# Graph layer on one core: the 64-byte tensor of exponents is allocated behind the statistics instead of ahead of the masks

## What is computed

```python
h = jnp.maximum(_layernorm(x, axis=-1), 0.0)
# in the layer, with _direction(x, W, Wg, b, bg, adj, rel_ids):
h = x @ W.T
g = h @ Wg.T
vals = (h[:, :, None, :] + b) * jax.nn.sigmoid(g[:, :, None, :] + bg)
onehot = (adj[..., None] == rel_ids).astype(h.dtype)
return jnp.einsum('bnmr,bmrd->bnd', onehot, vals)
# three directions (fwd, bwd: relations 2 to 40; loop: relation 1, on adj transposed)
x = x + jax.nn.relu(out)
```

## The kernel before

| tensor | bytes per partition | starts at | remainder by 128 |
|---|---|---|---|
| `x_all`, `adj_all`, `xn`, `hT_hi`, `hT_lo`, `gate` | 65536, 65536, 8192, 4096, 4096, 4096 | 16512 for `x_all`, the rest behind it | 0 |
| `vals` | 4096 | 168064 | 0 |
| `minus_half` | 64 | 172160 | 0 |
| `mask` | 8192 | 172224 | 64 |
| `stats` | 768 | 180416 | 64 |
| `var_eps`, `rstd`, `mean_neg` | 256 each | 181184, 181440, 181696 | 64 |
| `ident`, `ones`, `w_raw`, `w_gT`, `w_hi`, `w_lo`, `bias_all`, `zeros`, `bias_row`, `junk` | 512 to 8192 | 181952 for `ident`, the rest behind it | 64 |

## Time and profile before

### The profile page before, as it was taken

The page is one execution under the profiler, slowest core; times in us unless marked ns, Lnnn a source line. Parts: engine busy times, 40 slices in busy tenths (PEclk is TensorE's granted clock), DMA queues, the critical chain, the costliest instruction groups (busy, mean ns, idle before and its releaser), DMA issues.

```text
span 102.4 us, 2495 instructions
## 1 busy us (share of the span) xinstructions
PE 96.5 (94%) x802; PEld 92.5 (90%) x802; DVE 90.3 (88%) x197; ACT 90.3 (88%) x148; POOL 83.8 (82%) x158
## 2 busy tenths in 40 slices
PE   5988899999999999999999999999999999999960
PEld 2657798999999999999999999999999999999950
DVE  2289899999999999999999999999998588877661
ACT  5068889989999999999999989998999989898890
POOL 2275999999999999999999999999999999960000
PEclk9999999999999999999999999999999999999999
DMA  2899999999999999999999999999933341506345
GB/s 63 249 313 292 293 290 290 293 294 288 274 313 304 321 321 324 301 324 333 335 328 333 317 339 322 304 312 312 315 100 109 92 113 55 156 15 197 102 137 170
DMA packets 50288, 25.45 MB, mean 249 GB/s; under 512 B 866, under 2 KB 50276, under 8 KB 50276
## 3 DMA queue, kind: packets, MB, share of 16 engines
q1 hardware_dynamic: 50000, 25.17, 88.0%
q10 hardware_dynamic: 276, 0.13, 0.4%
HBM read 16.91 MB, written 8.39 MB: 247 GB/s over the span
## 4 chain that ended last, share of the span: by engine, by line
PE 80%; DMA 7%; DVE 4%; SPq 3%; ACT 3%; issue 1%
PE psum L827 25%; PE psum L805 14%; PE psum L806 14%; PE psum L810 14%; PE psum L792 13%; DMA x_all<-in_x 7%; ACT junk L467 2%; SPq L253 2%; DVE stats L554 1%; DVE xn L571 1%; DVE vals L587 1%; DVE hT_lo L597 1%; SPq L269 0%; SPq L270 0%; ACT gate L461 0%
## 5 line engine op out<-in xcount | busy, mean ns | idle before, releaser
L366 POOL TENSOR_SCALAR xn<-x_all,mean_neg,rstd 128x128 f32<-128x128 f32 x96 | 42.4, 456 | 0.5 <-issue 0.3
L805 PE MATMUL psum<-w_hi,hT_hi 128*128 128x256 f32 x128 | 34.3, 301 | 0.7 <-ACT hT_hi L427 0.3
L434 ACT ACTIVATE psum<-bias_all 128x1024 f32<-128x1024 f32 x32 | 33.0, 1032 | 0.7 <-DVE vals L587 0.6
L827 PE MATMUL psum<-vals,mask 128*128 128x128 f32 x256 | 33.6, 275 | 0.0
L806 PE MATMUL psum<-w_lo,hT_hi 128*128 128x256 f32 x128 | 31.6, 280 | 0.0
L827 PEld LDWEIGHTS psum<-vals,mask 128*128 128x128 f32 x256 | 31.1, 191 | 0.0
L554 DVE BATCH_NORM_STATS2 stats<-x_all 128x6 f32<-128x256 f32 x64 | 24.0, 420 | 3.5 <-DMA x_all<-in_x 3.5
L587 DVE TENSOR_TENSOR vals<-psum,gate 128x512 f32<-128x512 f32 (+1 forms) x33 | 21.9, 665 | 4.0 <-ACT gate L461 3.8
L805 PEld LDWEIGHTS psum<-w_hi,hT_hi 128*128 128x128 f32 x128 | 24.1, 188 | 1.5 <-issue 0.9
L348 POOL TENSOR_TENSOR rstd<-var_eps,minus_half 128x16 f32<-128x16 f32 (+2 forms) x11 | 24.5, 2224 | 0.1
L806 PEld LDWEIGHTS psum<-w_lo,hT_hi 128*128 128x128 f32 x128 | 24.2, 189 | 0.0
(11 more groups left out here) (38 smaller groups left out, 34.5 us busy)
## 6 DMA issues: line engine op xcount, KB each, us to landing
adj_all<-in_adj SPq DMA_DIRECT2D x16, 512.0 KB, 6.5
x_all<-in_x SPq DMA_DIRECT2D x15, 512.0 KB, 6.7
out<-x_all SPq DMA_DIRECT2D x14, 512.0 KB, 6.3
out<-x_all SPq DMA_DIRECT2D x3, 256.0 KB, 2.3
x_all<-in_x SPq DMA_DIRECT2D x2, 256.0 KB, 3.0
out<-x_all ACTq DMA_DIRECT2D x1, 128.0 KB, 2.5
out<-x_all SPq DMA_DIRECT2D x1, 128.0 KB, 2.6
w_raw<-in_L_gnn_W_loop SPq DMA_DIRECT2D x1, 64.0 KB, 2.4
```

The source lines that it names most:

```text
L366: last = pool.tensor_scalar(xn[:, g % XN, j * D:j * D + D], x_all[:, g * GC + j * D:g * GC + j * D + D], mean_neg[:, b % BATCH_SLOTS, k:k ...
L434: nc.scalar.activation(prod_ps[s].rearrange("p g a d -> p g (a d)"), bias_all[:, :, :].rearrange("p a d -> p (a d)").unsqueeze(1) .to_broa ...
L805: nc.tensor.matmul(to, hi, w_hi[:, :], start=False, stop=False, skip_group_check=True)
L827: last = nc.tensor.matmul(to[:, j * D:j * D + D], mask[:, g % MASKS, j * N:j * N + N], vals[:, s, j * D:j * D + D], start=True, stop=True)
```

## The change

One `sb(...)` line moves down by five lines. `minus_half` is no longer allocated between `vals` and `mask` but behind `mean_neg`.

```diff
         gate = sb("gate", [128, 2, GC])
         vals = sb("vals", [128, 2, GC])
-
-        minus_half = sb("minus_half", [128, BATCH])
         mask = sb("mask", [128, MASKS, GROUP * N])
         stats = sb("stats", [128, BATCH_SLOTS, BATCH // 2, 6])
         var_eps = sb("var_eps", [128, BATCH_SLOTS, BATCH])
         rstd = sb("rstd", [128, BATCH_SLOTS, BATCH])
         mean_neg = sb("mean_neg", [128, BATCH_SLOTS, BATCH])
+        minus_half = sb("minus_half", [128, BATCH])
         ident = sb("ident", [128, 128])
```

## The result

| | before | after |
|---|---|---|
| median | 104.19 us (7 runs) | 103.30 us (7 runs, 102.89 to 104.02) |
| ratio | | 0.9922, 95% interval 0.9903 to 0.9941 |
| the profiled execution | 104.14 us | 104.02 us |
| span in the profile | 102.4 us | 102.2 us |

The change makes the kernel 0.8% faster. The prediction named the masks' new place as worth nothing and forecast the old time, 104.3 us, so it is wrong, although 103.3 us lies within its range.

A forecast was written before the change was run, and what follows sets the result against it. The prediction took the pace at which PE starts its records as the bound. All terms were 0: 104.14 + 0 us against the profiled execution, 104.29 + 0 = 104.3 us as median, range 103.2 to 104.9 us.

The forecast's parts named there:

- the masks' new place: Masks at remainder 0 instead of 64, for PE's loads and ACT's and POOL's writes: forecast to change the time by 0.
- ACT's and POOL's masks: Writes of `mask`: term 0, staying at 640 ns on ACT and 0.61 us on POOL.
- the powers: POOL's powers for the statistics of each batch: 2.90 us each in slots at either remainder, term 0.
- the statistics' place: Slots of stats, var_eps, rstd and mean_neg only swap which has which remainder: term 0 on both ends.
- The slower rival: Aggregation: both operands at one remainder get into each other's way, 7.0 ns per record, 1.8 us, 106.1 us; chance 0.10.
- The last sign of being wrong: Profile after: wrong if PE's pace moves in any line, above all one whose operands did not move.
- The change part by part: Pricing of four kinds of access to moved tensors, each by its time at remainder 0 against 64; sum 0.
- PE's loads of `mask`: 256 aggregation loads, 191 ns against 188 at remainder 0, hidden behind multiplies: term 0, bounds 1.1 us gain, 1.8 us cost.
- the faster rival: Aggregation: loads of `mask` set its pace and remainder 0 frees it, 0.8 us, 103.5 us, at most 1.1 us; chance 0.14.
- slowest pace of the steady state: The products' 118 ns per record, used to price the loads' bad end and the slower rival at 1.8 us.
- The limit by the other engines: Steady state: POOL needs 10.84 us for four groups where PE needs 10.97, so the faster rival ends at 103.2 us.
- no change: Whole kernel: time the same within about 0.5%, what a measurement can tell; chance 0.76.

The follow-up runs named there:

- c2_stats_clean: Kernel before with stats, var_eps and rstd moved to remainder 0, mean_neg to the end; masks, ident and weights stay: 104.35 us, ratio 0.9991.
- c1_after_copy: The changed kernel unchanged, timed once more against the kernel before: 103.65 us, ratio 0.9936.
- c5_read_0: Kernel before, with PE loading the aggregation's stationary operand from an unchanging tensor of ones at remainder 0, masks still written at 64: 103.44 us, ratio 0.9907.
- c3_light_after: Changed kernel with less work: ACT's test reads 128 of 1024 columns, DVE's late statistics and POOL's late powers halved: 103.11 us, ratio 0.9879 to before.
- c1_mask_only: Kernel before with only the masks moved to remainder 0, statistics and all behind them staying in place: 103.38 us, ratio 0.9917.
- c5_read_64: Kernel before, with PE loading the aggregation's stationary operand from an unchanging tensor of ones at remainder 64, masks still written at 64: 104.35 us, ratio 1.0006.
- c1_stats_only: Kernel before with the statistics moved to remainder 0 and masks kept; its second gap also moved ident and weights by 128 bytes: 103.34 us, ratio 0.9908.
- run 113: Not a run label: "run" is a verb here, and 113 is the time in ns between the starts of matmul records.
- c2_weights_up128: Kernel before with 128 unused bytes ahead of ident, moving ident, weights and all behind them; masks and statistics stay: 103.28 us, ratio 0.9881.
- c3_light_before: Kernel before with less work: ACT's test reads 128 of 1024 columns, DVE's late statistics and POOL's late powers halved: 104.28 us, ratio 0.9979.

## Why the prediction was wrong

**What held.** PE's records set the time; the loads of `mask` (191 ns), the aggregation (0.89 us per eight records), ACT's and POOL's masks and the powers stayed as forecast; the statistics' place costs nothing (c2_stats_clean, 0.9991). The slower rival's mechanism is not there: records of the aggregation are as far apart as before. The last sign of being wrong that the prediction gave, that PE's pace moves in a line whose operands did not move, is the one that came.

**The step that failed** stands at the head of "The change part by part": "The change can cost or give something only where an engine's access takes another time at remainder 0 than at 64." It prices each moved operand at the instructions that read it. The runs showed a second way: the address of the aggregation's stationary operand decides at which of two paces the following products run. The term "PE's loads of `mask`" was put at 0, and for the loads and the aggregation that was right; the missing term stood on lines with no moved operand, the products, and had been put at nothing without a reason: 19 groups x 0.05 us, some 0.95 us, of which 0.75 us arrived. The time of the faster rival, 103.5 us, came out near the measured one by luck, for its mechanism did not: it has the aggregation's eight records at 0.86 or 0.87 us, and they are at 0.89.

**The reason for trusting the products' 118 ns** was that I had taken it for a property of the line, as the "slowest pace of the steady state". The trace of before had the sign against it, and I did not ask. These are the products of the first and of the second group in PE's timeline of before (start, us, what):

```profile
9.32 0.28 PE L806 MATMUL psum<-w_lo,hT_hi 128*128 128x256 f32 x1
...
10.00 0.28 PE L806 MATMUL psum<-w_lo,hT_hi 128*128 128x256 f32 x1
...
12.27 0.28 PE L806 MATMUL psum<-w_lo,hT_hi 128*128 128x256 f32 x1
...
12.98 0.28 PE L806 MATMUL psum<-w_lo,hT_hi 128*128 128x256 f32 x1
```

Six steps take 0.68 us in the first group (113 ns) and 0.71 in the second (118 ns), for the same instruction on the same tensors, one buffer further on. A line with two paces has a state, and a change that leaves the line alone can still move the state.

**The limit by the other engines** exists, but the prediction laid it on the wrong engine. It let PE gain no more than down to POOL's 10.84 us for four groups. With short groups PE needs 4 x 2.69 = 10.76 us, and from 57.30 to 81.54 us it keeps that for nine groups without a wait for POOL, whose powers stand at 62.68 and 73.49 us, 10.81 us apart. The products that waited, at 49.43 and 81.94 us, each start 0.14 us behind the end of ACT's write of the biases into their accumulators (timeline of after: start, us, what; the chain counts the same two products only from 49.57 and 82.14 us, where the transposes ahead of them are done):

```profile
48.26 1.03 ACT L433 ACTIVATE psum<-bias_all 128x1024 f32<-128x1024 f32 x1
...
49.43 0.36 PE L804 MATMUL psum<-w_hi,hT_hi 128*128 128x256 f32 x1
```

```profile
80.74 1.06 ACT L433 ACTIVATE psum<-bias_all 128x1024 f32<-128x1024 f32 x1
...
81.94 0.36 PE L804 MATMUL psum<-w_hi,hT_hi 128*128 128x256 f32 x1
```

The waits at the first product in c1_after_copy (60.19 us) and c5_read_0 (71.12 us) end in the same way, 0.14 to 0.15 us behind ACT's biases. Each time ACT had read a chunk for its test just before; in c3_light_after, where that read is short, there is no such wait from 35 us on, although DVE is relieved only from 51 us and POOL only from 62 us. Behind each of the two waits of after the group that waited and the two next run at 118 ns. The two waits cost 0.14 us themselves, and the six long groups behind them, by my estimate, 6 x 0.05 = 0.3 us of what the faster pace could have given.

**The chances.** 0.76 for no change rested on comparisons of durations row by row. None of them could show a state that is carried from one group to the next. The rule on 16-byte lines from the Trainium skill, page "SBUF — State Buffer", section "Door 1: The DMA port swizzle", would have the masks gain nothing from a start at 0; c1_mask_only, at 0.9917, shows that it does not give the whole effect of an address on PE. Its other rule, two independent read ports for PE in the section "Who interferes with whom", has nothing in it by which a load's address changes a later multiply; c5_read_0 against c5_read_64 shows such a change, 0.9 us.

## What to carry to other kernels

Where PE streams back to back, compare the starts of equal records from group to group, not their mean durations: two paces of one line meant here that its time depended on what ran before it, and on addresses. If a kernel is bound by PE and its matmuls sit at the longer pace, moving one operand's tensor by 64 or 128 bytes is a cheap trial with a possible 1%, but where to put it has to be found by trying; "a multiple of 128" is not it. A gap or a moved small tensor shifts all that is allocated behind it, so an experiment on one tensor has to hold the addresses of the others, as c1_stats_only did not.

## What was not expected of the hardware

- Matmuls of 256 f32r columns, each with a load of 128x128 f32, run 113 or 118 ns apart at a granted clock of 1.00, with loads of 188 ns in both; in before and after the pace holds for all twelve products of a group and mostly from group to group. With `ident` and the weights 128 bytes further on, a group turns to 113 ns after two products (c2_weights_up128).
- Without waits PE's rhythm repeats to within a ns. In the kernel before three groups repeat in turn, although POOL and DVE repeat every four groups (one batch), and they do so in c3_light_before too, so the rhythm seems to be PE's own. With the masks at remainder 0 the sequence 202, 205 of the first product's step is followed by 200 and the 113 ns; with 64 it goes 204, 202 (or 201), 201 and round again.
- At which of its address bits PE's reading is sensitive, and by what the pace is handed on, stays open: four addresses of the masks and three of the weights were tried, and none of the runs looks into PE. With the weights in place, the two stationary addresses at remainder 0 (172160, 198784) brought many short groups, and the three at 64 and the one at 32 at most two.
